# Three attention cores of a decoder layer: the turned row maxima leave through ScalarE's DMA queue, one exponential later, and the value loads of the causal cores are issued later

## What is computed

```python
x = x + _L0_attn_ref(_layernorm(x, axis=-1), L0_attn_w_qkv, L0_attn_w_out)
x = x + _L0_xattn_ref(_layernorm(x, axis=-1), ctx_1024, fside_BxSx2_0, fside_BxSx2_0, ...)
x = x + _L0_ffn_ref(_layernorm(x, axis=-1), ...)   # rotary attention, then 8 experts, top 2
...
scores = jnp.einsum('bqhd,bkhd->bhqk', q, k)
scores = jnp.where(causal_mask[None, None], scores, NEG)
attn = jax.nn.softmax(scores, axis=-1)
out = jnp.einsum('bhqk,bkhd->bqhd', attn, v).reshape(b, s, HIDDEN)
```

## Time and profile before

| what | value |
|---|---|
| median of three runs | 2305.2 us (2299.11 to 2305.41) |
| the profiled execution's own time | 2297.42 us |
| its span, first to last instruction | 2295.6 us |
| mean granted TensorE clock | 0.938 |
| PE, DVE, ACT, POOL busy | 90%, 54%, 38%, 31% |
| ACT in the cross core, 620 to 1050 us | 290.50 of 430.00 us |
| PE in the cross core, 620 to 1050 us | 396.49 of 430.00 us |

### The profile page before, as it was taken

One profiled execution on the slowest core, in us unless ns is written; L12 is line 12 of the kernel. 1 busy time (PEld: TensorE's weight loads), 2 busy tenths in 40 slices (PEclk: granted clock), 3 DMA queues, 4 the chain that ended last, 5 costly groups with the idle time before them and its releaser, 6 DMA issues. The chain is left out here.

```text
span 2295.6 us, 31417 instructions
## 1 busy us (share of the span) xinstructions
PE 2069.8 (90%) x10679; PEld 1384.3 (60%) x10679; DVE 1237.3 (54%) x2679; ACT 881.1 (38%) x1662; POOL 708.3 (31%) x610
## 2 busy tenths in 40 slices
PE   6998999887689999996987999979999988999998
PEld 5775666565433434334776666657788877565664
DVE  5446656377689788875976656534313142222221
ACT  3335444343368676773334544433212210111111
POOL 0004555346513232322554654511000000233332
PEclk9997999989789999998997999889999998999999
DMA  5557666345654545443457665453012043433332
GB/s 188 172 192 174 140 136 136 113 163 217 254 127 100 132 116 152 103 124 117 179 192 227 151 152 128 102 200 110 30 63 74 1 172 117 142 60 59 63 65 36
DMA packets 149937, 297.14 MB, mean 129 GB/s; under 512 B 23762, under 2 KB 42324, under 8 KB 148756
## 3 DMA queue, kind: packets, MB, share of 16 engines
q1 hardware_dynamic: 113972, 243.73, 36.6%
q10 hardware_dynamic: 27072, 32.77, 5.3%
q0 software_dynamic: 8736, 18.62, 4.3%
HBM read 181.55 MB, written 102.50 MB: 124 GB/s over the span
## 5 line engine op out<-in xcount | busy, mean ns | idle before, releaser
L1157 ACT ACTIVATE cross_c_prob<-bank 128x512 f32<-128x512 f32 x512 | 271.3, 598 | 124.4 <-PE bank L996 123.4
L1194 DVE TENSOR_REDUCE cross_c_row_max<-bank 128x2 f32<-128x1024 f32 x256 | 300.0, 1212 | 34.8 <-PE bank L965 29.0
L996 PE MATMUL bank<-stack 56*128 56x512 f32 (+4 forms) x768 | 238.7, 437 | 34.1 <-DMA stack<-first_c_max_rows 11.4
L1577 PE MATMUL bank<-moe_hT,moe_w 128*128 128x512 f32 x1056 | 261.5, 405 | 2.2 <-DVE moe_hT L1819 2.2
L965 PE MATMUL bank<-stack 48*128 48x512 f32 (+4 forms) x768 | 218.1, 465 | 36.1 <-PEq L70 19.5
L1577 PEld LDWEIGHTS bank<-moe_hT,moe_w 128*128 128x128 f32 x1056 | 206.5, 197 | 47.3 <-DVE moe_hT L1819 2.6
L996 PEld LDWEIGHTS bank<-stack 56*128 56x128 f32 (+1 forms) x768 | 122.6, 198 | 164.8 <-ACT cross_c_prob L1157 70.3
L1665 PE MATMUL bank<-moe_w_e,moe_hT_e 128*128 x624 | 195.0, 466 | 1.6 <-DMA moe_w_e<-in_experts_packed 1.2
L965 PEld LDWEIGHTS bank<-stack 48*128 48x128 f32 (+1 forms) x768 | 107.4, 206 | 123.6 <-DVE cross_c_row_max L1194 51.7
L1190 DVE CUSTOM_DVE_ANT_0 first_c_masked<-bank,later 128x128 f32<-128x128 f32 (+3 forms) x256 | 115.8, 486 | 88.5 <-PE bank L965 87.6
L1190 DVE CUSTOM_DVE_ANT_0 rotary_c_masked<-bank,later 128x128 f32<-128x128 f32 (+3 forms) x256 | 116.0, 486 | 85.8 <-PE bank L965 84.9
(11 more groups left out here) (344 smaller groups left out, 3967.8 us busy)
## 6 DMA issues: line engine op xcount, KB each, us to landing
moe_w_e<-in_experts_packed SPq DMA_DIRECT2D x8, 2176.0 KB, 9.0
qk_parts<-first_p_parts SPq DMA_DIRECT2D x32, 512.0 KB, 2.7
stack<-qk_parts SPq DMA_DIRECT2D x64, 256.0 KB, 6.9
qk_parts<-cross_p_parts SPq DMA_DIRECT2D x32, 512.0 KB, 2.7
stack<-qk_parts SPq DMA_DIRECT2D x256, 64.0 KB, 2.4
qk_parts<-rotary_p_parts SPq DMA_DIRECT2D x32, 512.0 KB, 2.7
moe_raw<-in_shared_packed SPq DMA_DIRECT2D x11, 768.0 KB, 11.5
stack<-qk_parts SPq DMA_DIRECT2D x16, 512.0 KB, 5.1
```

The source lines that it names most:

```text
L996: last = nc.tensor.matmul(bank[:, 0 : S - q0], k_stack[slot][r : r + ALL_ROWS, at, m * P : (m + 1) * P], q_stack[slot][r : r + ALL_ROWS, a ...
L1157: nc.scalar.activation(probability(g, step // HEADS_AT_ONCE, step % HEADS_AT_ONCE), psum[bank_at["score", n]][:, 0 : S - q0], ACT.Exp).the ...
L1194: nc.vector.tensor_reduce(row_max[:, g % 2, m, j - 1 : j + 1], c.banks[:, first : first + WIDE, :], AX_X, ALU.max).then_inc(s.max_done, 1)
L1577: last = nc.tensor.matmul(psum[bank][:], weights(pa, f, k), hT[p % 2][:, pb, k, :], start=m == 0, stop=m == len(steps) - 1)
```

## The change

`send_max` is called on ACT. It stands behind `take_max(0)` for group 0, and for each later group behind the exponential of step `MAX_STEP` + 1, so that one exponential lies between the copy into `max_rows` and the DMAs. SP's list loses `send_max`; the stores that it divided into early and late ones are one list now. The value loads of first and rotary move from step 6 to step 11. The value loads of cross and all residual loads stay where they were.

```diff
-                def send_max(sp, g):
-                    sp.wait_ge(s.max_rows, g + 1)
+                def send_max(act, g):
+                    act.wait_ge(s.max_rows, g + 1)
                     for half in range(HALVES):
                         r = half * HALF_ROWS
-                        sp.dma_start(q_stack[g % STACK_SLOTS][r + PRODUCT_ROWS : r + ALL_ROWS].bitcast(F32),
+                        act.dma_start(q_stack[g % STACK_SLOTS][r + PRODUCT_ROWS : r + ALL_ROWS].bitcast(F32),
                                      max_rows[:].bitcast(F32).unsqueeze(1).to_broadcast([2 * HEADS_AT_ONCE, PER_HALF, S])).then_inc(s.max_loaded, 16)
...
-                    send_max(sp, 0)
                     for g in range(GROUPS):
...
-                        early = [m for m in stores_now if OUT_AT[m][-1][1] < MAX_STEP]
-                        for m in early:
+                        for m in stores_now:
                             store(sp, (g // G - 1) * TT + m)
-                        if g + 1 < GROUPS:
-                            send_max(sp, g + 1)
-                        for m in stores_now:
-                            if m not in early:
-                                store(sp, (g // G - 1) * TT + m)
...
                     take_max(0)
+                    send_max(act, 0)
...
                             if step == MAX_STEP and g + 1 < GROUPS:
                                 take_max(g + 1)
+                            if step == MAX_STEP + 1 and g + 1 < GROUPS:
+                                send_max(act, g + 1)
...
-                            if causal and step == 6 and g + V_SLOTS - 1 < GROUPS:
+                            if causal and step == 11 and g + V_SLOTS - 1 < GROUPS:
                                 load_values(act, g + V_SLOTS - 1)
```

## The result

| what | before | after |
|---|---|---|
| median of the compared runs | 2302.15 us (4 runs) | 2321.19 us (4 runs, 2317.42 to 2322.38) |
| ratio, 95% interval | | 1.0082 [1.0056, 1.0108] |
| the profiled execution, its span | 2297.42, 2295.6 us | 2317.42, 2315.6 us |
| mean granted TensorE clock | 0.938 | 0.937 |

The change makes the kernel 0.8% slower, 19.0 us between the medians and 20.0 us between the profiled spans. The forecast was slower, +13.3 us (2318 us, range 2300 to 2334).

The account below looks back on a forecast made before the run. In cross PE and DVE were taken as nearly full, ACT in a loop with PE. Terms 10.2 + 6.5 - 1.0 - 1.1 - 2.0 + 0.7 = +13.3 us: profiled 2297.4 to 2310.7, laid on the median 2318 us, range 2300 to 2334.

Parts of the forecast that it names:

- ACT's issues in cross: Two issues on ACT delay exponentials that PE waits for: 0.33 us in each of 31 groups, +10.2 us (0 to +31).
- about 0.15 us of this is covered: Cross, PE's product of step 15: part of its 0.47 us delay hides because it queues behind its pair's first, leaving 0.33.
- ACT's issues in first and rotary: One 0.73 us issue a group fits in the next exponential's 1.59 us wait for PE: 0, at most 11 us.
- The queue in cross group 2: Maxima now stand behind the residual load on ACT's queue, so PE starts the next group at about 685.5: +6.5 us.
- The other four places: Cross's queue elsewhere: group 13 -1.0 us, group 10 -1.1; groups 18, 21 and 29 change by 0.2 at most.
- Queue and value loads in first and rotary: Maxima ahead of value loads, behind residuals: first group 2 -2.0 us, group 7 +0.7; four like places 0, each within 1.
- The start of a core: One more stack's loads precede the first maxima, now behind 1 MB of weights on ACT's queue: 0, up to +5 a core.
- Rival 1: ACT's issues in cross are hidden, leaving only the queue's +3.1 us: 2308 us, chance 0.25.
- rival 2: Maxima land early everywhere: first and rotary gain 17 us, cross 7.6, less ACT's 10.2, giving -15: 2290 us, chance 0.11.
- rival 3: ACT's stall counts in full, 1.0 us in each of 31 cross groups: +34 us, 2339 us, chance 0.13.

Follow-up runs that it names:

- e1: Changed kernel with cross's maxima, group 0's too, back on SP, first and rotary still on ACT: 1.0034 of the kernel before.
- e3: Changed kernel, but in cross ACT issues one of the two maxima DMAs and SP the other: 1.0037 of the kernel before.
- e4: Kernel before, maxima still on SP, plus two spare DMAs of the same shape on ACT in each cross group but the last: 1.0081 of the kernel before.
- e7: Changed kernel with residual loads at step 12 instead of 4 and cross's value loads at step 12 instead of 2: 1.0005 of the kernel before.
- e8: Kernel before with residual loads and cross's value loads at step 12, value loads of first and rotary at step 11: 0.9893 of the kernel before.
- e11: Kernel before, residual loads at step 12 (cross's first in group 4, not 2), first and rotary value loads at step 11, cross's unchanged: 0.9876 of the kernel before.
- e6: Changed kernel with the value loads of first and rotary back at step 6: 1.0134 of the kernel before.
- e2: Changed kernel, but SP waits for the first maxima before loading stack 3, as in the kernel before: 1.0074 of the kernel before.
- e5: Changed kernel with only the first maxima of each core back on SP, ahead of stack 3's loads: 1.0082 of the kernel before.
- e12: e8 a second time, run beside e11 on one chip: 0.9915 of the kernel before.
- e9: Kernel before, as e8, but cross's value loads at step 12 of groups 5, 13 and 21: 0.9986 of the kernel before.

## Why the prediction was right in direction and too small

**The number.** The forecast, 2318 us, lies close to the 2321.2 measured, but this is partly luck. Against the traces two terms were 15.7 us too low together (5.3 of ACT's issues, 10.4 of the starts), and the others were 9 us too high together.

**ACT's issues in cross: the mechanism right, the term mis-sized, 15.5 us instead of 10.2.** The pair of issues costs 1.46 us as assumed, the exponential of step 11 starts 1.2 us later behind that of step 10 than before (1.14 walked through), and e1, e3 and e4 show from three sides that the issue time makes the short groups longer. The step that failed is the last one, "about 0.15 us of this is covered": in the short groups nothing was. The exponential of step 12 is 0.49 us late (0.47 walked through), the weight load of step 15 0.48 and the next group 0.49. In the groups with a projection step 12 is 0.63 us late (0.6 walked through) and 0.13 of it was covered, which also gives 0.50 instead of 0.33. The term has a threshold, as the working said: e3, with one issue of 0.70 us, lost nothing.

**ACT's issues in first and rotary, 0: right.** Groups 4 to 6 of first take 12.27, 17.96 and 17.88 us where they took 12.27, 17.95 and 17.88.

**The queue in cross group 2: right in kind, 2.5 us instead of 6.5.** PE started 0.8 us behind the landing of the residual, where the term had 0.1. But the residual landed 14.7 us behind its issue instead of 18.8, so there was less to wait for. The other four places, -2.1 in the sum, gave -4.7: groups 14 and 21 were taken as unchanged or nearly so and are both better. Group 14 gained without a wait of its own: behind the shorter wait ahead of it (1.34 instead of 2.77 us) it ran at a granted clock of 1.00 instead of 0.86, a price of late maxima that the working left out. In the experiments cross group 2 took 18.71 to 21.19 us with maxima on ACT, so one trace fixes this term only within 1 or 2 us. Of the two sections of the Trainium skill's page "DMA: Bandwidth & Descriptors" that the prediction weighed, "Queues, rings and completion order" agrees with the 0.8 us behind the residual and with the longer waits of cross group 3 in all runs with the maxima on ACT (the same section also says that completion is not first in, first out for an issuing engine, and e7, with the maxima 2.5 us ahead of the earlier residual, agrees with that), and "Issuing engines are not separate DMA queues" agrees with e7 against e8 and with e11, where the queue made little or no difference. Neither alone gives all the numbers here.

**Queue and value loads in first and rotary: -1.3 expected, -1.8 measured, by luck.** Without the two slow-clock groups first gives -1.7 and rotary -0.1. But in first only -0.2 of it lies where the working had its terms: the wait ahead of group 3 fell by 0.8 us (2.60 to 1.77), not 2.0, and that ahead of group 8 rose by 0.56 (0.7 expected). Groups 0 and 1, behind the later start of the core, are 1.4 us shorter, which the working did not have. e6 shows that without the later value loads these waits would be 5.0 us longer.

**The start of a core: taken at 0, measured +10.4.** This is the largest error of the forecast, and here the step that failed is the choice of 0. The working named both causes, the loads of one more stack ahead and the place behind ACT's loads, with up to 5 us a core as the bound (measured: 2.1, 3.4 and 4.9), and then chose 0 without a row for it. PE's waits of 5.41 and 4.52 us at these places stood in the trace of before and said that the first maxima were already late there, with nothing in PE's rows to cover a further delay. e2 and e5 share the 10.4 into 3.8, 4.8 and 1.8; that the total time follows them is not shown.

**The rivals.** Rival 1 (issues hidden) fell with 11.40 us groups, rival 2 (early landings everywhere) with waits of 1.77 to 4.11 us that stayed, rival 3 (1.0 us a group) with 0.50.

The sum that the traces give: 15.5 (issues) + 10.4 (starts) + 2.5 - 4.7 (cross's queue) - 1.8 (first and rotary) = 21.9; with 0.6 less in other cross groups and 1.3 less between the cores, 20.0.

## What to carry to other kernels

Before a DMA is moved to an engine that stands in the loop, multiply its issue time by the number between two instructions that PE waits for, and compare that with the engine's slack there: one issue of 0.7 us cost nothing here and two cost 0.5 us a group. For a small transfer that PE waits for, look at how many megabytes are under way when it leaves before looking at its queue: moving the large loads behind it gave about 1% without touching the maxima (0.9% in e12, 1.2% in e11, where they are also apart). If they can't be moved, keep it off their queue: behind a load that left 4 us earlier, sharing the queue cost about 3 us more. Count a wait of PE with what its clock then costs, about 3 us here in the groups behind waits of 2 to 4 us. Price the start of a phase apart from its steady state, since there nothing covers a late transfer.

## What the runs showed of the hardware

**An issue's cost goes more by the transfer than by the engine.** The transfer from 8 partitions takes 0.697 us to issue on ACT and 0.740 on SP in e3; an output store of 128 partitions took 0.338 us on SP and a lone residual load 0.37 to 0.39 on ACT. The Trainium skill, page "DMA: Bandwidth & Descriptors", section "Why a DMA increments its semaphore by 16 and not by 1", says that a DMA whose outer dimension is 8 runs on 8 of the 16 DMA engines and that the issuing sequencer then writes the missing 8 increments itself. That would be a reason for a dearer issue; no run here varied the partitions alone, so it is not shown. Nor is the shape all: the same residual load took 0.37 us alone (e11) and 0.52 right behind the value load (e7, e8, e9), and the first maxima of the first core took 1.33 us on ACT in after.

**Small transfers delay each other.** With two pairs at once the maxima landed 2.9 us behind the end of the issue instead of 1.7 (short groups of e4).

**A wait of PE can be paid twice, since the clock falls behind it.** TensorE's clock has two levels here, 1.2 and 2.4 GHz, and the granted clock of a stretch is their mix. In before and after, groups 3, 8 and 12 of first and of rotary begin behind a wait of PE of 1.8 to 4.1 us. Ten of these twelve groups take 15.1 to 16.1 us, at a granted clock of 0.78 (0.72 for the longest), and two take 19 us at 0.57. At a clock of 1.00 such a group takes 12.3. Group 12 of first in before, behind a wait of 3.72 us, and in e8, behind one of 0.77:

```profile
376.38:391.63 15.25, 14.88 (x100) 9.68 (x101) 8.39 (x31) 7.10 (x17) 5.26 (x4) 0.78 0.60 118
```

```profile
365.23:377.53 12.30, 11.93 (x100) 8.20 (x100) 8.37 (x33) 7.02 (x17) 8.00 (x7) 1.00 0.93 224
```

So a wait of 2 to 4 us costs about 3 us more in the group behind it, and this is a large part of what e8 gains. In first it takes 225.1 us from group 0 to 15 instead of 238.4. Of these 13.2 us, 8.7 are groups 3, 8 and 12 at full clock (12.3 to 12.4 us each, without the wait at their end), and 4.3 are PE's waits ahead of groups 1 to 15, 5.2 us in all instead of 9.5. The length of the wait alone does not decide it. Group 4 of first ran at 0.78 behind 1.53 us in e7, and at 1.00 behind 1.57 us in e8.

At 0.57 it was one group in before (group 12 of rotary, behind 3.18 us), one in after (group 8 of first, behind 3.73) and four in e6. Why one group falls to 0.57 and others, behind waits as long, to 0.78 is not shown. A single trace can be 4 us off for each of them, and the budget above takes them out by name.
